# A two-layer graph-attention kernel: the loop over pairs of iterations written out as straight code on every engine

## What is computed

```python
h = relu(layernorm(x)); x = x + gat(h, adj, W, a)         # layer 0
h = relu(layernorm(x)); x = x + gnn3(h, adj, ...)         # layer 1
# gat: Wh = h @ W; e = leaky(Wh@a1 + (Wh@a2).T), masked by adj; softmax;
#      keep the 16 largest of each row; elu(attention @ Wh)
# gnn3, for l in 0..2: scores = leaky(si + sj.T + b), masked by adj + I; softmax;
#      agg = attn @ x; h = layernorm(x + agg)
#      x = layernorm(h + gelu(h @ W1 + b1) @ W2 + b2)
```

## Time and profile before

| | us |
|---|---|
| median of 3 runs | 2914.31 (2912.55 to 2914.35) |
| the profiled execution | 2913.98 |
| its span, first to last instruction | 2912.3 |
| PE busy | 2752.7 (95%) |
| ACT busy | 2350.6 (81%) |
| POOL busy | 2313.8 (79%) |
| DVE busy | 2026.0 (70%) |

### The profile page before, as it was taken

How to read it: one execution, slowest core, us unless ns; L and a number is a source line. 1 busy time by engine, 2 the same in 40 slices (tenths; PEclk the granted TensorE clock), 3 DMA queues, 4 the chain that set the end, 5 groups by cost and what they waited for, 6 DMA issues and landing times.

```text
span 2912.3 us, 58716 instructions
## 1 busy us (share of the span) xinstructions
PE 2752.7 (95%) x17636; PEld 2474.2 (85%) x17636; DVE 2026.0 (70%) x7283; ACT 2350.6 (81%) x4767; POOL 2313.8 (79%) x2410
## 2 busy tenths in 40 slices
PE   4689999999999999999999999999999999999995
PEld 3578998888888898988889898888888999999874
DVE  4767777767777777777777777776777777676542
ACT  3577888888898888888888888888888888887663
POOL 0466888888888888888888888888888888888874
PEclk9899999999999999999999999999999999999997
DMA  4100011101101101101110110111110111010001
GB/s 150 46 28 26 25 34 25 34 20 34 33 27 25 35 20 34 34 26 34 25 35 20 34 32 28 25 34 20 34 35 25 34 25 34 20 30 19 10 10 15
DMA packets 96432, 89.72 MB, mean 31 GB/s; under 512 B 9120, under 2 KB 94368, under 8 KB 96032
## 3 DMA queue, kind: packets, MB, share of 16 engines
q1 hardware_dynamic: 79136, 68.32, 7.6%
q0 software_dynamic: 16896, 16.78, 4.4%
HBM read 47.34 MB, written 37.75 MB: 29 GB/s over the span
## 4 chain that ended last, share of the span: by engine, by line
PE 79%; DVE 12%; issue 4%; ACT 3%; POOL 1%; SPq 0%; DMA 0%; DVEq 0%; POOLq 0%; ACTq 0%
PE ps_ff L1120 11%; PE ps_ff L1122 10%; PE ps_ff L1121 10%; PE ps_mm L1101 10%; PE ps_mm L1099 10%; PE ps_mm L1100 10%; PE ps_ag L1157 5%; PE ps L1233 4%; PE ps_ht L1171 3%; PE ps L1223 2%; DVE U L893 1%; PE ps_s L1145 1%; DVE H L1005 1%; DVE st_y_six L789 1%; PE ps_s L1134 1%
## 5 line engine op out<-in xcount | busy, mean ns | idle before, releaser
L418 POOL TENSOR_TENSOR a_lo<-A,a_hi 128x512 fp32r<-128x512 f32 x576 | 776.1, 1350 | 347.3 <-ACT a_hi L541 334.9
L1120 PE MATMUL ps_ff<-w_hi,a_hi 128*128 128x256 f32 x3072 | 900.6, 293 | 26.3 <-DVE a_lo L995 14.6
L1121 PE MATMUL ps_ff<-w_lo,a_hi 128*128 128x256 f32 x3072 | 853.5, 278 | 0.0
L1122 PE MATMUL ps_ff<-w_hi,a_lo 128*128 128x256 f32 x3072 | 852.8, 278 | 0.0
L533 ACT ACTIVATE A<-ps_mm,b_col 128x512 f32<-128x512 f32 x768 | 521.7, 683 | 319.9 <-PE ps_mm L1101 191.9
L1099 PE MATMUL ps_mm<-ht_hi,w_hi 128*128 128x512 f32 x1536 | 630.8, 411 | 4.8 <-ACT A L533 3.4
L1120 PEld LDWEIGHTS ps_ff<-w_hi,a_hi 128*128 128x128 f32 x3072 | 577.4, 188 | 54.8 <-DVE a_lo L995 17.3
L1101 PE MATMUL ps_mm<-ht_lo,w_hi 128*128 128x512 f32 x1536 | 607.0, 395 | 0.0
L1100 PE MATMUL ps_mm<-ht_hi,w_lo 128*128 128x512 f32 x1536 | 604.2, 393 | 0.0
L1121 PEld LDWEIGHTS ps_ff<-w_lo,a_hi 128*128 128x128 f32 x3072 | 578.5, 188 | 18.4
L1122 PEld LDWEIGHTS ps_ff<-w_hi,a_lo 128*128 128x128 f32 x3072 | 578.1, 188 | 0.0
(11 more groups left out here) (113 smaller groups left out, 5129.8 us busy)
## 6 DMA issues: line engine op xcount, KB each, us to landing
xr<-in_x SPq DMA_DIRECT2D x32, 512.0 KB, 3.9
out<-x SPq DMA_DIRECT2D x32, 512.0 KB, 2.9
out<-H POOLq DMA_DIRECT2D x32, 512.0 KB, 6.1
mask_in<-mask_park SPq DMA_DIRECT2D x96, 128.0 KB, 2.4
adj_sb<-in_adj SPq DMA_DIRECT2D x32, 256.0 KB, 2.9
mask_park<-mask_out SPq DMA_DIRECT2D x32, 128.0 KB, 1.7
X<-in_L_gnn_W SPq DMA_DIRECT2D x3, 1024.0 KB, 5.7
H<-in_L_gnn_W SPq DMA_DIRECT2D x3, 1024.0 KB, 6.7
```

What stands on the lines that cost most here:

```text
L418: pool.tensor_tensor(a_lo[:, at], A[:, at], a_hi[:, at].bitcast(F32), ALU.subtract).then_inc(s["a_lo_gpsimd"], 1)
L1120: pe.matmul(out_g, a_hi[:, at, cols], w2_hi[:, l, m], start=first, stop=False, skip_group_check=True)
L1121: pe.matmul(out_g, a_hi[:, at, cols], w2_lo[:, l, m], start=False, stop=False, skip_group_check=True)
L1122: last = pe.matmul(out_g, a_lo[:, at, cols], w2_hi[:, l, m], start=False, stop=final, skip_group_check=True)
```

## The change

In schedule(), the loop is replaced by the same iterations written out, for each of the five engines. As k is then always an integer, value(), seq(), chunks_before() and the others give constants, and settle() emits nothing. No other line differs.

```diff
@@ -237,9 +237,8 @@
             for i in range(FIRST, FIRST_STEADY):
                 iteration(i)
-            with eng.Fori(0, (LAST_STEADY + 1 - FIRST_STEADY) // 2) as j:
-                iteration(At(j, 2, FIRST_STEADY))
-                iteration(At(j, 2, FIRST_STEADY + 1))
+            for i in range(FIRST_STEADY, LAST_STEADY + 1):
+                iteration(i)
             for i in range(LAST_STEADY + 1, LAST):
                 iteration(i)
```

## The result

The changed kernel took 2873.97 us (median of 4 runs, 2872.0 to 2875.4) against 2913.43 for the kernel before in the same comparison: ratio 0.9866, 95% interval 0.9849 to 0.9883. The forecast was 2874.5 with a range of 2869.5 to 2882.5. The profiled execution took 2874.61 us (span 2872.8) against 2913.98.

A forecast was written before the change was run, and what follows sets the result against it. TensorE, busy 95% of the span, bounds the kernel. Its removable loss of 14.1 + 13.7 + 7.2 + 0.9 + 3.7 = 39.6 us takes 2913.98 to 2874.4, called 2874.5; range 2869.5 to 2882.5.

The forecast's parts named there:

- (a): VectorE's ten jumps back go, 2.46 us of "issue" at one; PE's ten mm2 waits for a_lo, 13.7 us, become zero.
- (b): PE's own ten jumps back go, with the "issue" gaps ahead of a trip's first matmul: 7.2 us.
- the 108 ns: The Trainium skill's compare-and-branch time, estimated at 1.1 us for ten PE jumps; the prediction used the measured gaps instead.
- (c): Register waits become constant waits; z_topk's L893 lose 1.03 us, and PE's 22 turn_z waits, 14.1 us, go.
- the same reading of L940: L940, directly behind a register wait, has its median at 678 ns in the loop and 230 in straight code.
- The prediction's own margin: In straight code L893 ends 0.8 us before PE's turn_z transpose; the loop's added 1.03 us eats that.
- (d): Longer first matmuls after PE waits go: 84.31 us busy per interval against 84.15 straight, 3.7 us in 23.
- (e): Added instruction fetching of straight code costs nothing; settle()'s increments and the loop counter add no separate term; DMAs unchanged.
- The rivals: z_topk wait partly stays, 0.05; edge gaps are not the jump's, 2895 us, 0.03; straight code stalls, 2947 us, 0.02.
- The first: Over many straight iterations turn_z still waits for z_topk; 2889 us if all 14.1 stays, 2881.5 if half; chance 0.05.
- The slower rival: PE's sequencer stalls 0.72 us at each of about 100 new code blocks, 72 us; 2947 us; chance 0.02.

The follow-up runs named there:

- the probe: All engines straight; VectorE ran extra loops at the end: bodies of 8, 100 and 600 tiny instructions, and waits of each kind; 3155.52 us, extra loops included.
- two probes: All engines straight plus extra VectorE loops at the end: tiny instructions and waits, 3155.52 us; in the other, copies of z_topk's end, 2903.33 us.
- the increment: Kernel before, loop kept everywhere, one semaphore increment (settle) added on VectorE behind z_topk's last register wait; 2937.68 us, ratio 1.0082.

## Why the prediction was right

**The place and the total: right.** The straight iterations at both ends of the kernel before were the control, and the middle went to their pace. 84.15 us was expected for an iteration, 84.01 came, 23 x 0.14 = 3.2 us better; the start and the end gave 3.4 back. Two misses of over 3 us cancel, and that the forecast came within half a microsecond is luck to that extent.

**(a) and (b), the jumps: the mechanism right, the shares mis-sized.** The waits of 13.7 and 7.2 us were added as if each belonged to its engine. VectorE straight alone left 18.0 us at PE's jump, not 7.2; PE straight alone won 8.8. They lie side by side, and their sum holds only because both went. Refusing the 108 ns was right: the probe has 2.6 to 2.9 us for a long body.

**(c), the register waits: the size right, the mechanism wrong.** "The four L893 behind it take 2.17 us" since the wait is against a register: this step failed, and with it the same reading of L940. The long instruction is the fourth, held by a GpSimd instruction that started first; register waits as such took nothing in two probes. The prediction's own margin should have warned: 1.03 us against 0.8 leaves a wait of 0.23 us, 5 us in 22 waits and not 14.1. With the lateness of 0.46 us on top it comes near the 0.64 us for each that the row has. The loop's own contribution is half a microsecond of lateness, which decides who is first. The 14.1 us went all the same, because straight code put VectorE back ahead.

**(d), restarts: as predicted**, since the pace of PE's busy time fell with the idle time (84.31 to 83.99 us for an interval).

**(e), reading the code: right.** 9 packets on q8 and 9 on q14 from 813.80 to 985.76, against 11 and 18; no PE gap at any block. ScalarE's ten gaps cost PE nothing, as taken: PE and VectorE straight give 2874.67 with ScalarE looped. SyncE's and GpSimd's loops likewise, but only in that company: with VectorE late, straight GpSimd cost 10 us.

**The rivals.** None happened. The first was argued from VectorE's lateness against turn_z; the margin is in fact only 0.05 us against GpSimd in the iteration shown. Where it is missed in every iteration, PE's waits come to 14.1 us (the kernel before), and with a second instruction held to 27.9 (the increment). No L893 in the middle of the changed kernel missed it, but one in the first probe did. The chance of 5% was thus smaller than the ground under it deserved. The slower rival, reading straight code, is refuted by the empty list of PE's waits.

## What to carry to other kernels

Where a kernel has peeled iterations beside a loop, compare their pace before anything else: it gives the worth of unrolling with its sign. A jump back over a long body cost 2.5 us on VectorE, 1.8 on PE and 1.1 on ScalarE here, and the stalls of different engines overlap, so unroll all engines on the critical path together; here PE and VectorE were enough, and one alone brought under half. When a VectorE instruction is sometimes four times as long, look at what GpSimd started just before it, before blaming the instruction's own waits. When a kernel loses more than its waits add up to, look at the granted clock behind the longest of them.

## What the runs showed of the hardware

A jump on VectorE: 0.04 to 0.06 us over a body of 8 instructions, 2.6 to 2.9 us over one of 600; on PE 1.8 us where nothing covers it. VectorE instructions with two SBUF operands took 1.37 us in place of 0.35 when a 128x512 GpSimd instruction of 1.3 us had started 0.1 us earlier, and stayed at 0.35 inside a 128x4 GpSimd instruction of 1.02 us. A VectorE copy of 0.68 us, started 0.03 us ahead, lengthened GpSimd's 1.02 us to 1.52. One semaphore increment for an iteration on VectorE cost 24 us in all by shifting that order: 13.8 us more waits of PE at turn_z, and some 9 us from six stretches of 3.4 us at the 1.2 GHz level, each right behind a wait of 1.9 us. Five other such waits had no fall behind them.
